# Dense experts: the second layer in seven products, its sums on GpSimd, VectorE's sums joined

## The reference, cut to what matters

```python
w = softmax(feat @ Wr + br)                       # 8 weights for each node
h = relu(_bn(einsum('bfd,edh->bfeh', x, W1) + b1, g1, be1, m1, v1))
h = relu(_bn(einsum('bfeh,ehk->bfek', h, W2) + b2, g2, be2, m2, v2))
y = einsum('bfeh,ehd->bfed', h, Wo) + bo
x = x + einsum('bfed,fe->bfd', y, w)              # all 8 experts, all nodes, float32
```

## Time and profile before

| | us |
|---|---|
| median of three runs | 6481.54 |
| profiled execution, its own time | 6477.92 |
| profiled execution, span | 6476.1 |
| busy: TensorE | 4835.1 (75%) |
| busy: VectorE | 4589.5 (71%) |
| busy: ScalarE | 1866.7 (29%) |
| busy: GpSimd | 3756.2 (58%) |
| mean granted clock of TensorE | 0.872 of full |

### The profile page before, as it was taken

How to read it: one execution, slowest core, us unless ns; L and a number is a source line. 1 busy time by engine, 2 the same in 40 slices (tenths; PEclk the granted TensorE clock), 3 DMA queues, 4 the chain that set the end, 5 groups by cost and what they waited for, 6 DMA issues and landing times. The chain is left out here.

```text
span 6476.1 us, 92397 instructions
## 1 busy us (share of the span) xinstructions
PE 4835.1 (75%) x21948; PEld 3568.6 (55%) x21949; DVE 4589.5 (71%) x9241; ACT 1866.7 (29%) x5236; POOL 3756.2 (58%) x3925
## 2 busy tenths in 40 slices
PE   1457777777677664599867777767778777999999
PEld 1345555555555553399634444445555555666666
DVE  8988887887887778723567666666776777565555
ACT  8322322222222222244420000012222215333333
POOL 0117777777777776155247777777777774222222
PEclk9967888888888887699978888887887788999999
DMA  1012222222222222322455545455555543000001
GB/s 60 17 46 55 58 57 57 57 57 57 57 58 56 58 58 65 112 70 71 144 146 141 140 139 138 138 141 147 147 147 146 148 137 98 5 5 8 6 5 40
DMA packets 383798, 532.70 MB, mean 82 GB/s; under 512 B 123405, under 2 KB 244258, under 8 KB 383522
## 3 DMA queue, kind: packets, MB, share of 16 engines
q0 software_dynamic: 139648, 299.92, 18.8%
q1 hardware_dynamic: 244002, 231.21, 11.8%
HBM read 473.88 MB, written 56.96 MB: 82 GB/s over the span
## 5 line engine op out<-in xcount | busy, mean ns | idle before, releaser
L886 POOL DMA_INDIRECT got<-table,st_idx x3232 | 3085.9, 955 | 1010.4 <-issue 902.5
L964 PE MATMUL ps_sum<-weighted,hot 128*128 128x260 f32 x6464 | 1827.4, 440 | 175.0 <-DVE acc L1036 171.3
L964 PEld LDWEIGHTS ps_sum<-weighted,hot 128*128 128x128 f32 x6464 | 1365.5, 223 | 586.7 <-DVE acc L1036 266.1
L1036 DVE TENSOR_TENSOR acc<-acc,ps_sum 128x260 f32 x1664 | 707.1, 425 | 733.4 <-PE ps_sum L964 585.4
L949 PE MATMUL ps_score<-score_split,hot_t 128*128 x3232 | 242.8, 184 | 968.2 <-DVE z L1016 944.5
L1028 DVE TENSOR_TENSOR weighted<-got,ps_weight 128x2048 f32<-128x2048 f32 x404 | 921.5, 2281 | 4.0 <-ACT weighted L924 0.8
L921 ACT ACTIVATE ps_weight<-z 128x32 f32<-128x32 f32 x404 | 81.3, 201 | 2624.5 <-DVE z L1016 2624.5
L949 PEld LDWEIGHTS ps_score<-score_split,hot_t 128*128 128x128 bf16 x3232 | 190.7, 100 | 1144.7 <-issue 1128.7
L987 DVE TENSOR_TENSOR hot<-ps_score,row_loc 128x1024 f32<-128x1024 f32 x404 | 492.1, 1218 | 3.5
L3068 POOL TENSOR_TENSOR x_sums<-acc 128x448 f32<-128x448 f32 x56 | 64.0, 1144 | 661.9 <-PE ps_hf L2989 661.8
L3023 PE MATMUL ps_yf<-ws_f,h2t 128*128 128x256 f32 x1568 | 347.7, 379 | 0.8 <-ACT h2t L3087 0.8
(11 more groups left out here) (550 smaller groups left out, 8329.1 us busy)
## 6 DMA issues: line engine op xcount, KB each, us to landing
spread<-row_list SPq DMA_DIRECT2D x404, 256.0 KB
got<-table,st_idx POOLq DMA_INDIRECT x3232, 2.7
gate_xin<-ball_rows SPq DMA_DIRECT2D x98, 128.0 KB
got_y_e<-y_rows SPq DMA_DIRECT2D x10, 896.0 KB
table<-row_e SPq DMA_DIRECT2D x50, 130.0 KB, 3.2
ball_rows<-xt SPq DMA_DIRECT2D x10, 640.0 KB, 4.7
mix_xin<-ball_rows SPq DMA_DIRECT2D x49, 128.0 KB
xn_rows<-xs_m SPq DMA_DIRECT2D x49, 128.0 KB, 1.7
```

Of the source, the lines that this page charges most:

```text
L886: pool.indirect_dma_start(got[:, r, k, :], None, table, bass.IndirectOffsetOnAxis(ap=st_idx[:, r, k:k + 1], axis=0))\
L964: last = nc.tensor.matmul(ps_g[:, p % 2, 0:AW], hot[:, r % 2, k, :], weighted[:, r % 2, k, :], start=(k == n * p), stop=(k == n * p + n - 1))
L1036: nc.vector.tensor_tensor(acc[:, ds(b * AW, AW)], acc[:, ds(b * AW, AW)], ps_g[:, p % 2, 0:AW], ALU.add).then_inc(added, 1)
```

## The change

1. The second layer uses the seven-product scheme too. GpSimd makes four more sums of the weights for each expert (`w_sums` has two layers now) and, for each step, four sums of the hidden values (`hidden_sums`), behind all four first-layer relus. Its order in a step is hidden sums, (weight sums of the next expert,) token sums of the next step.
2. `ps_hf` has six banks, in the order BANKS: the fourth product takes the first one's bank, all others have their own. `ps_yf` has two banks, with two output tiles in each.
3. VectorE adds up each layer in four instructions for seven: two sums of one bank, one over two quarters (the fourth product, broadcast), and one over three quarters and the three banks of products five to seven. It does so twice in a step.
4. ScalarE copies the first product of each layer into `part_sums`. Its order for each layer is copy, relu of the quarter (1,1), then three relus that all wait for the last sum.
5. VectorE's bias rows are spread between the sums: 0, then 1 and 2 inside the second layer's sums, 3, then 4 and 5 inside the first layer's, 6.

```diff
     EPS = 0.001
-    CUT = 4
-    HALVES = ((0, CUT * P), (CUT * P, (SUP - CUT) * P))
+    PRODUCTS, SUMS = 7, 4
+    BANKS = (0, 1, 2, 0, 3, 4, 5)
...
-        w_sum = sb("w_sums", [P, 2, 4, P])
-        first_p = sb("first_product", [P, half])
-        u_sum = sb("u_sums", [P, 3, half])
-        quarter = sb("quarters", [P, 4, half])
-        x_summed, w_summed = sem("x_summed"), [sem("w_even_summed"), sem("w_odd_summed")]
-        p_made, p_kept, u_made = sem("products_made"), sem("first_product_kept"), sem("quarters_made")
+        h_sum = sb("h_sums", [P, 4, half])
+        w_sum = sb("w_sums", [P, 2, 2, 4, P])
+        part = sb("part_sums", [P, 5, half])
+        quarter = sb("quarters", [P, 3, half])
+        x_summed, h_summed, w_summed = sem("x_summed"), sem("h_summed"), [sem("w_even_summed"), sem("w_odd_summed")]
+        made = [sem("first_layer_products"), sem("second_layer_products")]
+        kept = [sem("first_layer_kept"), sem("second_layer_kept")]
+        added = [sem("first_layer_sums"), sem("second_layer_sums")]
...
-        ps_y = own.enter_context(nc.psum_tensor("ps_yf", [P, 4, 512], F32))
+        ps_h = own.enter_context(nc.psum_tensor("ps_hf", [P, 6, 512], F32))
+        ps_y = own.enter_context(nc.psum_tensor("ps_yf", [P, 2, 512], F32))
+
+        def y_bank(k):
+            return ps_y[:, k // 2 % 2, k % 2 * D:(k % 2 + 1) * D]
         root, ready, chain = sem("bnf_root"), sem("bnf_ready"), sem("bnf_chain")
         biased, saved = sem("x_biased_f"), sem("saved")
...
+                def product(l, q, i, weights, right):
+                    nc.tensor.matmul(ps_h[:, BANKS[i], 0:half], weights, right, start=True, stop=True).then_inc(made[l], 1)
+
+                def w(par, l, c, f):
+                    return ws[:, par, l, c, f * P:(f + 1) * P]
+
+                def first_layer(q, par, s, alone=False):
+                    if not alone:
+                        pe.wait_ge(added[1], (q - 1) * SUMS + 3)
+                    product(0, q, 0, w(par, 0, 0, 0), x_part(s, 0, 0))
+                    pe.wait_ge(x_summed, q * 4 + 2)
+                    product(0, q, 1, w_sum[:, par, 0, 1, :], x_sum[:, 1, :])
+                    pe.wait_ge(x_summed, q * 4 + 3)
+                    product(0, q, 2, w_sum[:, par, 0, 2, :], x_sum[:, 2, :])
+                    pe.wait_ge(kept[0], q + 1)
+                    product(0, q, 3, w_sum[:, par, 0, 0, :], x_sum[:, 0, :])
+                    if not alone:
+                        pe.wait_ge(added[1], (q - 1) * SUMS + 4)
+                    product(0, q, 4, w(par, 0, 1, 0), x_part(s, 1, 0))
+                    pe.wait_ge(x_summed, q * 4 + 4)
+                    product(0, q, 5, w(par, 0, 1, 1), x_sum[:, 3, :])
+                    product(0, q, 6, w_sum[:, par, 0, 3, :], x_part(s, 1, 1))
+
...
                 def second_layer(q, par):
...
+                    pe.wait_ge(h_ready[0], q * 4 + 4)
+                    product(1, q, 0, w(par, 1, 0, 0), h_part(h1, 0, 0))
+                    pe.wait_ge(h_summed, q * 4 + 2)
+                    product(1, q, 1, w_sum[:, par, 1, 1, :], h_sum[:, 1, :])
+                    pe.wait_ge(h_summed, q * 4 + 3)
+                    product(1, q, 2, w_sum[:, par, 1, 2, :], h_sum[:, 2, :])
+                    pe.wait_ge(kept[1], q + 1)
+                    product(1, q, 3, w_sum[:, par, 1, 0, :], h_sum[:, 0, :])
+                    product(1, q, 4, w(par, 1, 1, 0), h_part(h1, 1, 0))
+                    pe.wait_ge(h_summed, q * 4 + 4)
+                    product(1, q, 5, w(par, 1, 1, 1), h_sum[:, 3, :])
+                    product(1, q, 6, w_sum[:, par, 1, 3, :], h_part(h1, 1, 1))
 
...
                 def step(pair, par, s, ahead):
 
                     q = (pair * 2 + par) * SUPS + s
-                    pe.wait_ge(h_ready, q * 8 + 8)
                     second_layer(q, par)
                     ahead(q + 1)
-                    pe.wait_ge(h_ready, q * 8 + 12)
+                    pe.wait_ge(h_ready[1], q * 4 + 4)
                     for k in range(SUP):
-                        pe.wait_ge(y_used, q * SUP + (k + 1))
+                        if k % 2 == 0:
+                            pe.wait_ge(y_used, q * SUP + (SUP - 1, SUP, SUP + 2, SUP + 4)[k // 2])
                         for c in range(2):
-                            last = nc.tensor.matmul(ps_y[:, k % 4, 0:D], h2[:, c, k * P:(k + 1) * P], ws[:, par, 2, c, :],
+                            last = nc.tensor.matmul(y_bank(k), h2[:, c, k * P:(k + 1) * P], ws[:, par, 2, c, :],
                                                     start=(c == 0), stop=(c == 1))
                         last.then_inc(y_made, 1)
...
+                def sums(link, to, part):
+                    of = [tiled(to[:, i, :]) for i in range(4)]
+                    link(nc.gpsimd.tensor_tensor(of[0], part(0, 1), part(0, 0), ALU.subtract))
+                    link(nc.gpsimd.tensor_tensor(of[1], part(1, 1), of[0], ALU.subtract))
+                    link(nc.gpsimd.tensor_tensor(of[2], part(1, 1), part(0, 1), ALU.subtract))
+                    link(nc.gpsimd.tensor_tensor(of[3], part(1, 0), of[1], ALU.subtract))
+
+                def token_sums(q, s, first=False):
                     if not first:
-                        pool.wait_ge(p_made, q * 7 - 1)
-                    link = Chain(pool, x_summed, 4, q)
-                    of = [tiled(x_sum[:, i, :]) for i in range(4)]
-                    link(nc.gpsimd.tensor_tensor(of[0], x_part(s, 0, 1), x_part(s, 0, 0), ALU.subtract))
-                    link(nc.gpsimd.tensor_tensor(of[1], x_part(s, 1, 1), of[0], ALU.subtract))
-                    link(nc.gpsimd.tensor_tensor(of[2], x_part(s, 1, 1), x_part(s, 0, 1), ALU.subtract))
-                    link(nc.gpsimd.tensor_tensor(of[3], x_part(s, 1, 0), of[1], ALU.subtract))
+                        pool.wait_ge(made[0], q * PRODUCTS - 1)
+                    sums(Chain(pool, x_summed, 4, q), x_sum, lambda c, hf: x_part(s, c, hf))
+
+                def hidden_sums(q):
+                    pool.wait_ge(h_ready[0], q * 4 + 4)
+                    sums(Chain(pool, h_summed, 4, q), h_sum, lambda c, hf: h_part(h1, c, hf))
+                weight_sums(0, 0)
+                token_sums(0, 0, True)
...
                 for e in range(EXPERTS):
-                    weight_sums(e // 2, e % 2)
                     for s in range(SUPS):
-                        token_sums(e // 2, e % 2, s, e + s == 0)
+                        q = e * SUPS + s
+                        hidden_sums(q)
+                        if s == SUPS - 1 and e + 1 < EXPERTS:
+                            weight_sums((e + 1) // 2, (e + 1) % 2)
+                        if q + 1 < EXPERTS * SUPS:
+                            token_sums(q + 1, (s + 1) % SUPS)
 
...
+                def layer(l, h, q, par, first=False):
+                    act.wait_ge(made[l], q * PRODUCTS + 1)
+                    if l == 1:
+                        act.wait_ge(added[0], q * SUMS + 4)
+                    elif not first:
+                        act.wait_ge(added[1], (q - 1) * SUMS + 4)
+                    nc.scalar.copy(part[:, 1, :], ps_h[:, BANKS[0], 0:half]).then_inc(kept[l], 1)
+                    act.wait_ge(added[l], q * SUMS + 3)
+                    relu(h, l, par, 1, 1, part[:, 4, :])
+                    act.wait_ge(added[l], q * SUMS + 4)
+                    relu(h, l, par, 0, 1, quarter[:, 2, :])
+                    relu(h, l, par, 0, 0, quarter[:, 0, :])
+                    relu(h, l, par, 1, 0, quarter[:, 1, :])
 
...
+                def expert(pair, par, final=False):
+                    with act.Fori(0, SUPS - 1) as s:
+                        q = (pair * 2 + par) * SUPS + s
+                        layer(1, h2, q, par)
+                        layer(0, h1, q + 1, par)
+                    q = (pair * 2 + par) * SUPS + (SUPS - 1)
+                    layer(1, h2, q, par)
+                    if not final:
+                        own_columns(pair + par, 1 - par)
+                        layer(0, h1, q + 1, 1 - par)
...
+                def quarters(l, q, between):
+                    def made_in(i):
+                        return ps_h[:, BANKS[i], 0:half]
+                    u2, u3 = part[:, 0, :], part[:, 2, :]
+                    dve.wait_ge(kept[l], q + 1)
+                    dve.wait_ge(made[l], q * PRODUCTS + 2)
+                    nc.vector.tensor_tensor(u2, part[:, 1, :], made_in(1), ALU.add).then_inc(added[l], 1)
+                    dve.wait_ge(made[l], q * PRODUCTS + 3)
+                    dve.wait_ge(added[l], q * SUMS + 1)
+                    nc.vector.tensor_tensor(u3, u2, made_in(2), ALU.add).then_inc(added[l], 1)
+                    between[0]()
+                    dve.wait_ge(made[l], q * PRODUCTS + 4)
+                    dve.wait_ge(added[l], q * SUMS + 2)
+                    if not (isinstance(q, int) and q == 0 and l == 0):
+                        dve.wait_ge(h_ready[1 - l], (q - 1 + l) * 4 + 1)
```

(70 more changed lines are left out.)

62 lines of the change are left out of this document (6 added, 56 removed).

## The result

The changed kernel takes 6665.77 us (median of 4 runs, 6664.64 to 6668.02) against 6483.1 for the kernel before (median of 4): ratio 1.0288, 95% interval 1.0276 to 1.0301. It is 183 us slower; 6685 was predicted, in a range of 6605 to 6740. The profiled execution took 6664.64 us, with a span of 6662.7 us.

The account below looks back on a forecast made before the run. TensorE alone was taken to bound the kernel. Per step -0.75+2.15+0.3+1.15 = +2.85 us, 157 over 55 steps; with 7+5+3, 172; with the clock's 34, +206: 6685 us, range 6605 to 6740.

Parts of the forecast that it names:

- Saving of 0.75 us a step: Second layer on TensorE: 16 passes taking 6.01 us become seven products taking 5.26 us, 42 us over 56 steps.
- Hole at the copy: TensorE waits before the fourth first-layer product for ScalarE's copy, queued behind three activations: 2.15 us a step with weight load.
- The three-bank sum 1.55 and the two-bank sum 1.08: VectorE's joined sums, durations in us read off a line between sums of 448 and 2048 columns.
- Hidden sums: GpSimd's sums of hidden values: the third comes late for the second layer's third product, a 0.3 us hole a step.
- Lock: VectorE's two-SBUF-input bias rows blocked by GpSimd's running sums, delaying the three-bank sum 1.15 us a step; bounds 0 to 1.5.
- T: Time mark in a step: the end of the seventh first-layer product, when TensorE's output products start.
- S: Time mark in a step: the end of the second layer on TensorE.
- R1: Rival: bias rows don't hold back the three-bank sum, hole 2.1 us, clock mostly holds; 6590 to 6620 us; chance 0.17.
- Clock: TensorE's granted clock falls after holes of about 3.3 us, costing 1.7 us of work each; 34 us in all.
- Half the steps: Clock falls counted in half the steps, since each lengthened step shortens the next hole to about 2.2 us.
- Rest: Costs outside the ordinary step: seven changes of expert at 1.0 us each (7), the start 5, the end 3 us.
- R4: Rival: faster, TensorE has no hole, 6440 us; even with the three-bank sum at 0.62, slower by about 45; chance 0.02.

Follow-up runs that it names:

- two experiments that remove it by different means: Against the changed kernel: ScalarE's first-layer copy moved ahead of the three activations, 6522.28 us; or three-bank sum split into three, each followed by its activation, 6542.02 us.

## Why the prediction was right, point by point

- Saving of 0.75 us a step: right. The seven second-layer products take 5.59 us in the step shown, with the wait for the hidden sum in them.
- Hole at the copy, predicted 2.15: right. TensorE's idle time is 1.97, and the first layer takes 5771.84-5764.24 = 7.60 for 5.26, so 2.34 with the exposed weight loads and the 0.17 by which the three-bank sum was late; 2.17 without that. Shown by two experiments that remove it by different means.
- The three-bank sum 1.55 and the two-bank sum 1.08: measured 1.554 and 1.079 in the mean of 112 each. The line between 448 and 2048 columns holds.
- Hidden sums, predicted hole 0.3: 5.59-5.26 = 0.33.
- Lock, predicted 1.15: wrong, 0.17 measured. Bias row 1 is held to the end of a GpSimd sum, as the prediction said (1.02 us), but row 2 was placed wrongly. With T = 5752.61 it was to start at T+11.6, behind the start of the third token sum (T+11.47 by the prediction's pitch of 1.22); it came at T+11.39, 0.16 us ahead of that sum. The two-bank sum of 1.08 us starts as row 1 ends, just behind the start of a GpSimd sum, so row 2 at 5764.00 comes just before that sum ends (5762.88+1.21 = 5764.09), is through in 0.47, and it is GpSimd that waits: 5764.16, 1.31 us for 1.14. In all 47 steps inside an expert the three-bank sum starts at S+0.32 to S+0.37. That row 1, held to the end of a GpSimd sum, sets this phase is an argument, not a test. It is the condition of rival R1, and the prediction's own sign of it, a period near 19 us ("no lock"), came: 19.23 us in the 18 steps inside an expert that have no fall.
- Clock, predicted 34: 49 in the steps, some more at changes of expert. The price of a fall, 1.7, was right to 0.01. "Half the steps" came near (29 of 47), but by luck: I had every second hole at 3.3 us and the others at 2.2. All are 1.92 to 1.97 and 29 of 47 bring a fall, where the earlier trace rows had shown falls behind 3.02 and 3.44 and none behind 1.62. What decides which of these equal holes bring one, no run here shows. These falls are also why R1's time, 6590 to 6620, did not come with its condition.
- Rest: changes of expert 2.5 us each for 1.0; the start 11.7 for 5 and one ordinary step's 1.9, since TensorE waited there for the hidden values (3.74 us) and for the first of their sums (1.46) and ran at the lower clock in two stretches (granted clock 0.50 from 5509.1 to 5515.8 and from 5522.8 to 5526.1); the end 2.6 for 3. In R4, "about 45" is 37 by its own terms (0.40 x 55 + 15); nothing hangs on it.

The prediction took the plain step (one without a fall) at 17.31+2.85 = 20.16 us; 19.23 came. The lock put its sum 53 us too high (54 x 0.98); the rest of the plain step, the clock, the changes of expert and the start put it 3+15+10+4 too low; together it came out about 20 us too high. That it came so near is in part luck: errors of opposite sign cancelled by more than half. The sign and the main mechanism were right, the fourth product held by a copy behind three activations that wait for one joined sum; the part of the lock was not, nor the reason given for how often the clock falls.

## What to carry to other kernels

Before joining sums or moving a copy, write down what stands behind them in their engine's order, and when each had been released before: a joined instruction releases all its readers at the time of its last input. Two waits that lie over each other have to be taken away together; alone each looks free. VectorE instructions with two SBUF inputs belong where GpSimd rests (seven rows took 2.86 us there and 5.25 beside its sums), and not in front of a sum that others wait for. Where a term hangs on the phase of two loops, it has two values and not one (here 0.17 or 1.08 us a step): price both.

## What the runs showed of the hardware

- An idle time of 1.97 us in front of dense work was followed by a fall of the clock from 2.4 to 1.2 GHz in 29 of the 47 steps inside an expert (32 of 47 with the weight sums made earlier), one of 0.47 us in none of 47, and one of 2.96 us in 30 of 47. With 2.96 us the granted clock from 5520 to 6440 us was 0.93, for 0.95 with 1.97 us and 0.99 with 0.47. Each fall in the changed kernel's steps cost 1.70 us.
- The lock between a bias row and a GpSimd sum goes both ways: the one that comes first makes the other wait (row 1.02 to 1.22 us for 0.48, GpSimd sum 1.31 for 1.14), to be seen in the rows of the steps above. The Trainium skill's SBUF — State Buffer, "Who interferes with whom", says that issue order decides who blocks; the trace agrees.
- What the lock costs thus depends on the phase of two loops: the three-bank sum was 0.17 us late in one order of rows, where the second row came 0.16 us ahead of a GpSimd sum, and 1.08 us late in the other, where it came 0.12 us behind the start of one (5920.20 and 5920.08).
- One VectorE sum with one operand in PSUM took 0.619 us for 448 columns, 1.079 for 896 and 1.554 for 1344 columns in three banks: no more than the line between 448 and 2048 columns gives.
